# Double-buffered normalised rows, table and choice steps spread among other vector work, last scatters two tiles earlier, in a fused attention and mixture-of-experts kernel

## The chip, the core and the metric

The kernel runs on one core of a Trainium2 chip. Its time is the device time of one execution in microseconds (us), the median of several runs. Five engines work at once: PE (matrix products), DVE (vector), ACT (scalar functions), POOL (GpSimd, which here mostly issues indirect DMAs) and SP (which issues most other DMAs). Each engine takes its instructions in order; engines meet through semaphores, counters that one instruction raises and another waits for.

## The reference, cut to what matters

```
x = L0_attn_x                                   # 4 sequences x 1024 tokens x 128, f32
x = x + attention(layernorm(x), w_lhs, w_rhs)   # scores (x*w_lhs)(x*w_rhs)^T, softmax over 1024 tokens, times layernorm(x)
h2 = layernorm(x)
probs = softmax(h2 @ router_w.T)                # 8 experts
gates, chosen = top_2(probs); gates /= gates.sum()
for each token and each of its 2 experts e:
    y += gate_e * (gelu(h2 @ w_fc[e] + b_fc[e]) @ w_proj[e] + b_proj[e])   # 128 -> 512 -> 128
x = x + y
```

## The kernel before, in words

The attention runs sequence by sequence ("batch" b = 0..3) on 128-token tiles, eight to a batch, in two "units" of four tiles (unit u = 2b, 2b+1). The second half is the mixture of experts, and its rows are sorted by expert. For each token the normalised row h2 is written as a float16 high and low part into `stage`, together with its two gates, its first expert and its number. POOL scatters these rows with indirect DMAs (`dispatch`, line 846) into a table in DRAM called `slots`, where each expert has a region of its own. A batch takes 16 scatters: 8 tiles of tokens, 2 experts each.

The regions are then read back in 47 tiles: 24 full ones of 256 rows, then 23 of 128. Which region and row a tile starts at is computed on DVE by `make_table`, a generator whose yields are its steps, and which `steps(table, n)` advances by n steps. It runs four times: `first_table` (tiles 0 to 7), `second_table` (8 to 15), `late_table` (16 to 23) and `small_table` (24 on). `table_made` counts the finished ones.

A tile k passes through the engines like this.

- SP `load` fetches its rows. The loads of tiles 8 to 15 wait for all scatters of batch 2 (`dispatched[0]`) and for the second table; those of tiles 16 on wait for the 16 last scatters, batch 3's.
- PE in its step k: `turn_slots(k+2)` (4 transposes, line 1352), `up(k)` (12 matmuls, lines 1365 to 1367), `down(k-2)` (16 matmuls, line 1386). `down(k)` waits for `biased_made` to reach k-1, since it writes the PSUM bank that `add_bias(k-2)` reads. In step 4, behind `down(2)`, comes `rank_round(last)`, which counts how many tokens of batch 3 chose each expert; `up(5)` and `down(3)` follow.
- ACT copies the transposed rows out of PSUM, does the gelu, and in its first steps makes h2 of the last two units (`make_h2`, `high_h2`).
- DVE in its step k: `keep_rows(k)` (5 small operations on the rows' gates and numbers), `add_bias(k-3)` (line 1844, waits until `up(k)` is done and so until PE is past `down(k-3)`), and `gate(k-3)` (line 1851).
- POOL `give_back(k-4)` in step k scatters the gated rows to `results` (line 950), two indirect DMAs for a full tile, one for a half tile; 71 in all.

In its steps 0 to 5 DVE also carries the routing of batch 3: statistics of unit 7 (`take_stats2`, `take_moments2`), `choose` (the generator `picks`, lines 1594 to 1615, which ends in `taken_made`, and so lets `rank_round` start), `find_gap`, `split_h2` (the low part of h2, line 1565), the second table, `keep_ranks(last)` and `find_slots(last)`. The last line of `find_slots`, 1662, raises `meta_made`, for which the last scatters wait on POOL. The queue of POOL around this is written out by hand: scatters of batch 2 in groups of 5, 6, 4 and 1 with other work between them, then the tiles' steps, with eight of the last scatters in step 6 and eight in step 7 (`LAST_SCATTERS`), ahead of that step's `give_back`.

At the end SP loads `results` once the results of all tiles are returned, DVE adds them to x, and x is stored.

Of the kernel before, what the change touches and what calls it, by code (L numbers as in the profile page):

```python
# [8 lines left out]
P = 128  # L9
F32 = mybir.dt.float32  # L10
# [13 lines left out]
def preln_attention_moe(nc, x, w_lhs, w_rhs, router_wT, w_fc, b_fc, w_proj, b_proj, out):  # L24
# [69 lines left out]
    with ExitStack() as ctx:  # L94
# [65 lines left out]
        h2 = sb("h2", [P, TU, D], F32)  # L160
# [580 lines left out]
        def _(pool):  # L741
# [201 lines left out]
            LAST_SCATTERS = {6: range(0, 8), 7: range(8, SCATTERS)}  # L943
# [21 lines left out]
        def _(act):  # L965
# [35 lines left out]
            def make_h2(u, t):  # L1001
# [7 lines left out]
                act.activation(h2[:, t, :], res[:, n, :], ACT.Identity, bias=bias, scale=scale).then_inc(h2_made, 1)  # L1009

            def high_h2(u):
# [6 lines left out]
                act.activation(high, h2[:, :, :], ACT.Copy).then_inc(h2hi_made, 1)  # L1018
# [79 lines left out]
            def step(k, a):  # L1098
# [320 lines left out]
        def _(dve):  # L1419
# [128 lines left out]
            def take_moments2(u):  # L1548
# [5 lines left out]
                ins.then_inc(ln2_moments, 1)  # L1554
                dve.wait_ge(ln2_moments, u + 1)
# [4 lines left out]
            def split_h2(u):  # L1560
# [4 lines left out]
                dve.tensor_tensor(part[:, :, D:2 * D], h2[:, :, :], part[:, :, 0:D], ALU.subtract).then_inc(h2lo_made, 1)  # L1565
# [73 lines left out]
            def find_slots(r):  # L1639
# [3 lines left out]
                for k in range(K):  # L1643
                    route_link(dve.tensor_tensor(pick[k][:, mine, :], pick[k][:, mine, :], rank[:, mine, :], ALU.mult))
                route_settle()
                for k in range(K):
                    ins = dve.tensor_reduce(slot_f[:, mine, k], pick[k][:, mine, :], AX_X, ALU.add)
                ins.then_inc(slots_made, 1)
                dve.wait_ge(slots_made, 4 * r + 1)
                dve.tensor_copy(slot[:, at, :], slot_f[:, mine, :]).then_inc(slots_made, 1)  # L1650
                dve.wait_ge(gate_exp, r + 1)
                route_link(dve.tensor_scalar(gate_sum[:, mine], gate2[:, mine], 1.0, None, ALU.add))
                route_settle()
                if b >= 2:
                    dve.wait_ge(dispatched[b % 2], 16 * K * BT * (b // 2))
                dve.reciprocal(rows[:, :, GATES], gate_sum[:, mine]).then_inc(slots_made, 1)
                dve.wait_ge(slots_made, 4 * r + 3)
                dve.tensor_tensor(rows[:, :, GATES + 1], rows[:, :, GATES], gate2[:, mine], ALU.mult).then_inc(slots_made, 1)
                dve.wait_ge(slots_made, 4 * r + 4)
# [26 lines left out]
            for b in range(B):  # L1686
# [86 lines left out]
                if b == B - 1:  # L1773
                    find_slots(ROUNDS_BY[b - 1] - 1)
# [41 lines left out]
            digits = {}  # L1816

            def keep_rows(k, a):
# [4 lines left out]
                if k >= NR:  # L1823
# [6 lines left out]
                                         op0=ALU.is_equal, op1=ALU.mult)  # L1830
                dve.scalar_tensor_tensor(out=gate_parts[:, a, 1, 0:n], in0=first_expert, scalar=e, in1=slot_rows[:, :, GATES + 1],
                                         op0=ALU.not_equal, op1=ALU.mult)
                dve.scalar_tensor_tensor(out=chosen_row[:, a, 0:n], in0=first_expert, scalar=e, in1=slot_rows[:, :, NUMBER],
# [93 lines left out]
```

## Time and profile before

| | |
|---|---|
| time, median of 3 runs | 307.52 us (306.63 to 308.74) |
| the profiled execution | 307.93 us, of which the span shown is 306.4 us |
| mean granted clock of PE in it | 0.964 of full speed |
| busy | PE 88%, DVE 77%, ACT 64%, POOL 59% |

The profiled execution is one of the runs' kind, 0.4 us above their median. Times in rows are us from the span's start. In rows that follow an engine through time ("timeline"), the columns are start, duration, engine, line of the code, operation, out<-in with sizes, and the count; a bracket at the end gives the engine's idle time just before the row and what ended it. Consecutive instructions of one form are joined into one row.

### The profile page before, as it was taken

Reading aid. Unit: us, or ns where it says so; the run is one execution under the profiler, and the core shown is the slowest. Engines: PE = TensorE matmul, PEld = TensorE weight load, DVE = VectorE, ACT = ScalarE, POOL = GpSimd, SP = SyncE. Lnnn points to the kernel's source line nnn. Section 1 sums busy time; section 2 is a strip of 40 time slices with the busy share of each in tenths; the row PEclk is TensorE's granted clock in tenths of the full one; section 3 lists DMA queues with packets and bytes.
Section 4 is the critical chain, followed back from the end, with each engine's and each line's share of the span. In section 5 each row is a group of like instructions: output and inputs, shape, how many; then the busy total and the mean of one; then the engine's idle time right before and its main releaser. Section 6 shows DMA issues by size and latency. Waiting matters only on the chain.

```text
span 306.4 us, 8241 instructions
## 1 busy us (share of the span) xinstructions
PE 270.9 (88%) x2223; PEld 242.1 (79%) x2223; DVE 236.1 (77%) x1002; ACT 196.4 (64%) x427; POOL 180.6 (59%) x245
## 2 busy tenths in 40 slices
PE   7899999899989998899989499988999999999500
PEld 2479898788969887689879499978999999998500
DVE  4699898889878769988979988897665655676655
ACT  2447378896369772545776667675778887898300
POOL 8111036017577782787757857777777777766600
PEclk9999999999999999999999689999999999999955
DMA  6960000000401100111241152213333333221886
GB/s 195 415 282 4 0 3 0 3 0 0 143 26 56 45 18 20 37 44 37 79 136 45 37 136 88 72 46 108 106 92 95 100 97 90 80 64 46 318 283 272
DMA packets 15450, 28.51 MB, mean 93 GB/s; under 512 B 3904, under 2 KB 9920, under 8 KB 15152
## 3 DMA queue, kind: packets, MB, share of 16 engines
q1 hardware_dynamic: 10224, 16.88, 16.8%
q0 software_dynamic: 4608, 10.07, 9.9%
q10 hardware_dynamic: 576, 1.05, 1.0%
q8 instruction: 20, 0.33, 0.4%
q14 instruction: 22, 0.18, 0.2%
HBM read 15.83 MB, written 12.16 MB: 91 GB/s over the span
## 4 chain that ended last, share of the span: by engine, by line
PE 56%; DVE 26%; issue 5%; ACT 5%; POOL 3%; DMA 3%; DVEq 1%; SPq 0%; POOLq 0%; ACTq 0%
PE av_ps L1386 16%; PE av_ps L1181 14%; DVE neg_piece L1502 5%; PE sc_ps L1365 3%; PE sc_ps L1367 3%; PE sc_ps L1366 3%; DMA raw_proj<-results 2%; PE sc_ps L1170 2%; PE bank L1352 2%; DVE h_all L1844 2%; PE bank L1157 2%; PE bank L1159 1%; PE bank L1158 1%; ACT h_all L972 1%; PE sc_ps L1158 1%
## 5 line engine op out<-in xcount | busy, mean ns | idle before, releaser
L950 POOL DMA_INDIRECT results<-prob,result_row x71 | 68.7, 968 | 27.4 <-issue 10.4
L1094 ACT ACTIVATE raw_fc<-sc_ps,bfc,scale_down 128x128 f32<-128x128 f32 (+1 forms) x188 | 81.6, 530 | 0.8 <-PE sc_ps L1367 0.8
L1386 PE MATMUL av_ps<-raw_proj,raw_fc 128*128 x568 | 74.5, 283 | 5.9 <-DVE h_all L1844 5.7
L846 POOL DMA_INDIRECT slots<-stage,slot x64 | 63.8, 997 | 25.7 <-issue 18.9
L1386 PEld LDWEIGHTS av_ps<-raw_proj,raw_fc 128*128 128x128 f32 x568 | 68.6, 196 | 8.0 <-issue 7.6
L1181 PE MATMUL av_ps<-h_all,prob 128*128 128x137 f32 x512 | 73.2, 285 | 0.6 <-DVE lg_part L1533 0.5
L1181 PEld LDWEIGHTS av_ps<-h_all,prob 128*128 128x128 f32 x512 | 66.8, 190 | 4.4 <-DVE res L1530 1.6
L1365 PE MATMUL sc_ps<-h_all,wfc_hi 128*128 128x128 f16 (+1 forms) x188 | 43.5, 248 | 1.1 <-ACT raw_fc L1094 1.1
L1366 PE MATMUL sc_ps<-h_all,wfc_hi 128*128 128x128 f16 (+1 forms) x188 | 43.5, 248 | 0.0
L1367 PE MATMUL sc_ps<-h_all,wfc_lo 128*128 128x128 f16 (+1 forms) x188 | 43.4, 247 | 0.0
L1844 DVE TENSOR_TENSOR h_all<-av_ps,bpr 128x256 f32<-128x256 f32 (+1 forms) x47 | 16.9, 360 | 28.7 <-PE sc_ps L1367 24.8
L1086 ACT ACTIVATE h_all<-bank 128x512 f16<-128x512 f16 (+1 forms) x47 | 23.4, 501 | 23.8 <-PE sc_ps L1367 23.3
L1502 DVE TENSOR_REDUCE neg_piece<-bank 128x1 f32<-128x512 f32 x32 | 22.0, 688 | 7.3 <-PE sc_ps L1170 3.5
L999 ACT ACTIVATE prob<-sc_ps 128x512 f32<-128x512 f32 x32 | 18.1, 599 | 10.0 <-PE sc_ps L1170 9.9
L989 ACT ACTIVATE again<-bank 128x512 f32<-128x512 f32 x16 | 9.6, 597 | 22.0 <-DVE neg_piece L1502 22.0
L1502 DVE TENSOR_REDUCE neg_piece<-sc_ps 128x1 f32<-128x512 f32 x32 | 21.9, 684 | 1.1 <-PE sc_ps L1159 1.0
L1365 PEld LDWEIGHTS sc_ps<-h_all,wfc_hi 128*128 x188 | 18.5, 98 | 2.8 <-issue 1.3
L1851 DVE TENSOR_SCALAR prob<-h_all,row_gate 128x128 f32<-128x128 f32 x71 | 19.1, 309 | 1.7
L1009 ACT ACTIVATE h<-res,shift,rstd 128x128 f32<-128x128 f32 x32 | 14.7, 489 | 8.3 <-DVE stage L1565 4.8
L1367 PEld LDWEIGHTS sc_ps<-h_all,wfc_lo 128*128 x188 | 18.5, 98 | 1.3
L1366 PEld LDWEIGHTS sc_ps<-h_all,wfc_hi 128*128 x188 | 18.5, 98 | 0.9
L1157 PE MATMUL bank<-hT_hi,q_hi 128*128 128x512 f32 x32 | 14.3, 448 | 1.6 <-DVE h_all L1461 1.3
(201 smaller groups left out, 524.5 us busy)
## 6 DMA issues: line engine op xcount, KB each, us to landing
slots_in<-slots SPq DMA_DIRECT2D x24, 132.0 KB
raw_fc<-in_w_fc_dram SPq DMA_DIRECT2D x1, 2048.0 KB, 10.9
raw_proj<-in_w_proj_dram SPq DMA_DIRECT2D x1, 2048.0 KB, 15.2
res<-in_x_dram SPq DMA_DIRECT2D x3, 512.0 KB, 5.8
slots_in<-slots SPq DMA_DIRECT2D x23, 66.0 KB
results<-prob,result_row POOLq DMA_INDIRECT x71, 2.3
slots<-raw_fc POOLq DMA_DIRECT2D x2, 528.0 KB, 4.1
slots<-stage,slot POOLq DMA_INDIRECT x64, 2.3
```

Source lines behind the costliest of these rows:

```text
L846: pool.indirect_dma_start(out=slots[:, :], out_offset=bass.IndirectOffsetOnAxis(ap=slot[:, n, k:k + 1], axis=0), in_=stage[:, b % 2, t, :] ...
L950: pool.indirect_dma_start(out=results[:, :], out_offset=bass.IndirectOffsetOnAxis(ap=result_row[a][:, h:h + 1], axis=0), in_=gated[a][h], ...
L1086: act.activation(xT[:, a % NH, 0:n], bank[a % 2][:, :].bitcast(F16)[:, 0:n], ACT.Copy).then_inc(xT_made, 1)
L1094: ins = act.activation(hid[:, a % NH, c, 0:halves_of(k) * P], up_ps(k, c), ACT.Gelu_apprx_tanh, bias=bfc[:, e, c:c + 1], scale=scale_down[ ...
L1157: pe.matmul(o, q_hi[:, a, rows], hT_hi[:, a, cols], start=True, stop=False, skip_group_check=True)
L1181: mm = pe.matmul(att[:, t, 0:AUG], probT[:, m % RING, t * P:(t + 1) * P], h_aug[:, b % 2, exp_rows(n), :], start=(n % BT == 0 and t % 2 == ...
L1365: pe.matmul(o, wfc_hi[:, e, of], xT[:, a % NH, 0:w], start=True, stop=False, skip_group_check=True)
L1366: pe.matmul(o, wfc_hi[:, e, of], xT[:, a % NH, w:2 * w], start=False, stop=False, skip_group_check=True)
L1367: mm = pe.matmul(o, wfc_lo[:, e, of], xT[:, a % NH, 0:w], start=False, stop=True, skip_group_check=True)
L1386: mm = pe.matmul(o, hid[:, a % NH, c, rows], wpr[:, e, c, :], start=(c == 0 and h == 0), stop=(c == HC - 1), skip_group_check=True)
L1502: dve.tensor_reduce(neg_piece[:, r // TU, r % TU, c:c + 1], block_bank(n), AX_X, ALU.max, negate=True).then_inc(max_made, 1)
L1844: dve.tensor_tensor(y, o, bpr[:, bass.ds(e, 1), :].to_broadcast([P, n, D]), ALU.add).then_inc(biased_made, 1)
```

## The change

1. `h2` gets two buffers, one for even and one for odd units. `make_h2(u)` waits for `split_h2(u-2)` in place of `split_h2(u-1)`; unit 7's four `make_h2` go two each to ACT's steps 2 and 3 (before, one each to steps 2 to 5).
2. DVE: `second_table` starts earlier, one step at a time inside `find_slots` of batch 2's last round and the statistics of units 6 and 7, and ends in step 0 (before, in step 4). The first read of the experts' numbers (`load_experts(0)`) moves ahead of `add_attention`. `choose` runs one step at a time between the operations of `keep_rows(1)` and `keep_rows(2)`. `find_gap(last)` comes at the end of step 2 and `split_h2(6)` at the start of step 2.
3. DVE, steps 3 to 5: `add_bias(k-3)` and `gate(k-3)` stand ahead of `keep_rows(k)`; in step 5 also ahead of `keep_ranks(last)` and `find_slots(last)`. `split_h2(7)` goes from step 7 to step 5. The late and small tables run one step at a time among `keep_rows` and `gate` of steps 6 to 9 and 10 to 13.
4. POOL: the scatters of batch 2 are grouped 6, 6, 3, 1, and the last 16 scatters come in steps 4 and 5, so `give_back(0)` follows the first eight and `give_back(1)` all sixteen.

The diff, cut to its core:

```diff
-        h2 = sb("h2", [P, TU, D], F32)
+        h2 = sb("h2", [P, 2, TU, D], F32)
...
-            for i in range(5):
+            for i in range(6):
                 dispatch(B - 2, i)
             scale_ln2(2 * B - 2)
-            for i in range(5, 11):
+            for i in range(6, 12):
                 dispatch(B - 2, i)
             scale_ln2(2 * B - 1)
-            for i in range(11, 15):
+            for i in range(12, 15):
                 dispatch(B - 2, i)
             gate_powers(len(ROUNDS) - 1)
...
-            LAST_SCATTERS = {6: range(0, 8), 7: range(8, SCATTERS)}
+            LAST_SCATTERS = {4: range(0, 8), 5: range(8, SCATTERS)}
...
-                if u >= 1:
-                    act.wait_ge(h2lo_made, u)
+                if u >= 2:
+                    act.wait_ge(h2lo_made, u - 1)
...
-                if 2 <= k < 6:
-                    make_h2(2 * B - 1, k - 2)
-                    if k == 5:
+                if 2 <= k < 4:
+                    for t in range(2 * k - 4, 2 * k - 2):
+                        make_h2(2 * B - 1, t)
+                    if k == 3:
                         high_h2(2 * B - 1)
...
-            def take_stats2(u):
+            def take_stats2(u, between=nothing):
                 dve.wait_ge(res_made, u + 1)
                 for t in range(TU):
+                    between()
                     ins = dve.bn_stats(stats2[:, u % 2, t, :], res[:, token_tile(u, t), :])
...
-            def find_slots(r):
+            def find_slots(r, between=nothing):
...
+                between()
                 route_settle()
                 for k in range(K):
                     ins = dve.tensor_reduce(slot_f[:, mine, k], pick[k][:, mine, :], AX_X, ALU.add)
                 ins.then_inc(slots_made, 1)
+                between()
...
                 if b == B - 1:
-                    find_slots(ROUNDS_BY[b - 1] - 1)
+                    dve.wait_ge(table_made, 1)
+                    second_table = make_table(dve, note, settle, 1)
+
+                    def second():
+                        steps(second_table, 1)
+                    find_slots(ROUNDS_BY[b - 1] - 1, second)
...
-                    take_stats2(2 * b)
-                    take_moments2(2 * b)
+                    take_stats2(2 * b, second)
+                    take_moments2(2 * b, second)
                     add_logits(2 * b)
 
-            dve.wait_ge(table_made, 1)
-            second_table = make_table(dve, note, settle, 1)
             steps(second_table, 8)
+            digits = {}
+            load_experts = expert_loader(dve, digits)
+            load_experts(0)
             add_attention(2 * B - 1)
...
+            STEPS = {0: second_table, 1: choose, 2: choose, 6: late_table, 7: late_table, 8: late_table, 9: late_table,
+                     10: small_table, 11: small_table, 12: small_table, 13: small_table}
+
+            def beside(k, n=1):
+                if k in STEPS:
+                    steps(STEPS[k], n)
...
                 if k == 0:
-                    take_stats2(2 * B - 1)
-                    take_moments2(2 * B - 1)
-                if 1 <= k < 4:
-                    steps(choose, (5, 5, 3)[k - 1])
-                if k == 3:
-                    find_gap(last)
+                    take_stats2(2 * B - 1, second)
+                    take_moments2(2 * B - 1, second)
+                if k == 2:
                     split_h2(2 * B - 2)
-                if k < 5:
-                    steps(second_table, (5, 6, 6, 4, 30)[k])
+                if 3 <= k < 6:
+                    add_bias(k - 3, (a - 3) % NB)
+                    gate(k - 3, (a - 3) % NB)
                 if k == 5:
                     keep_ranks(last)
                     find_slots(last)
-                if k == 7:
                     split_h2(2 * B - 1)
-                if 6 <= k < 10:
-                    steps(late_table, (7, 10, 10, 30)[k - 6])
-                if 10 <= k < 14:
-                    steps(small_table, (9, 9, 9, 30)[k - 10])
                 if tile_there(k):
                     keep_rows(k, a)
-                if k >= 3:
+                if k >= 6:
                     add_bias(k - 3, (a - 3) % NB)
+                    beside(k)
                     gate(k - 3, (a - 3) % NB)
+                beside(k, {0: 30, 1: 3, 2: 12, 6: 3, 7: 3, 8: 3, 9: 40, 13: 40}.get(k, 3))
+                if k == 2:
+                    find_gap(last)
```

The order that comes out on the engines, at three places. First, DVE around `keep_rows(0)` and `keep_rows(1)`. Before, `keep_rows` stands in one piece (the rows that write gate_parts, chosen_row, row_gate and result_row), then five steps of the choice (best, pick0, first_id0):

```order
L1829 SCALAR_TENSOR_TENSOR gate_parts<-slots_in,of_expert 128x2
L1831 SCALAR_TENSOR_TENSOR gate_parts<-slots_in,of_expert 128x2
L1833 SCALAR_TENSOR_TENSOR chosen_row<-slots_in,of_expert 128x2
L1836 TENSOR_TENSOR row_gate<-gate_parts 128x2
L1837 TENSOR_TENSOR result_row0<-chosen_row,spare_row 128x2
L1594 TENSOR_REDUCE best<-lg 128x8
L1597 TENSOR_TENSOR pick0<-lg,best 128x64
L1600 SCALAR_TENSOR_TENSOR pick0<-pick0,expert_id 128x64
L1604 TENSOR_REDUCE first_id0<-pick0 128x8
```

Now, in `keep_rows(1)`, the two alternate:

```order
L1853 SCALAR_TENSOR_TENSOR gate_parts<-slots_in,of_expert 128x2
L1601 TENSOR_REDUCE best<-lg 128x8
L1856 SCALAR_TENSOR_TENSOR gate_parts<-slots_in,of_expert 128x2
L1604 TENSOR_TENSOR pick0<-lg,best 128x64
L1859 SCALAR_TENSOR_TENSOR chosen_row<-slots_in,of_expert 128x2
L1607 SCALAR_TENSOR_TENSOR pick0<-pick0,expert_id 128x64
L1863 TENSOR_TENSOR row_gate<-gate_parts 128x2
L1611 TENSOR_REDUCE first_id0<-pick0 128x8
L1865 TENSOR_TENSOR result_row1<-chosen_row,spare_row 128x2
```

Each step of the choice needs the one before it, and now has an operation of `keep_rows` between itself and that one; in `keep_rows(0)` the steps between are the second table's.

Second, DVE from the gap of batch 3's gates (gap) to the first biases (h_all). Before:

```order
L1626 TENSOR_TENSOR gap<-step_down,rstd2 128x8
L1565 TENSOR_TENSOR stage<-h2,stage 128x4x128
L560 SCALAR_TENSOR_TENSOR tile_row<-sums,tile_at 128x8
L564 TENSOR_TENSOR of_expert<-of_expert,second_lane 128x8
L566 TENSOR_TENSOR tile_last<-tile_row,sums 128x8
L569 TENSOR_TENSOR skipped<-tile_row,tile_last 128x8
L1829 SCALAR_TENSOR_TENSOR gate_parts<-slots_in,of_expert 128x2
...
L1837 TENSOR_TENSOR result_row3<-chosen_row,spare_row 128x2
L1844 TENSOR_TENSOR h_all<-av_ps,bpr 128x256
```

Now:

```order
L1633 TENSOR_TENSOR gap<-step_down,rstd2 128x8
L1872 TENSOR_TENSOR h_all<-av_ps,bpr 128x256
L1880 TENSOR_SCALAR prob<-h_all,row_gate 128x128 x2
L1853 SCALAR_TENSOR_TENSOR gate_parts<-slots_in,of_expert 128x2
```

The split of h2, four table steps and `keep_rows(3)` no longer stand between the gap and `add_bias(0)`: the first two come earlier, the third behind it.

Third, POOL from the end of batch 2's scatters on (slots is a scatter of rows, results a `give_back`, gate<-euler,gap the gates of batch 3; the last number is the count). Before:

```order
L846 DMA slots<-stage,slot 32768x132 x4
L855 TENSOR_TENSOR gate<-euler,gap 128x8
L846 DMA slots<-stage,slot 32768x132
L950 DMA results<-prob,result_row 22528x128 x4
L846 DMA slots<-stage,slot 32768x132 x8
L950 DMA results<-prob,result_row 22528x128 x2
L846 DMA slots<-stage,slot 32768x132 x8
L950 DMA results<-prob,result_row 22528x128 x65
```

Now:

```order
L846 DMA slots<-stage,slot 32768x132 x3
L855 TENSOR_TENSOR gate<-euler,gap 128x8
L846 DMA slots<-stage,slot 32768x132 x9
L950 DMA results<-prob,result_row 22528x128 x2
L846 DMA slots<-stage,slot 32768x132 x8
L950 DMA results<-prob,result_row 22528x128 x69
```

The first of the last sixteen scatters now follows batch 2's last one directly, where four give-backs stood between; the number of calls is the same.

## Rows read from the trace of the kernel before

**Rows 1.** The page, busy time of each engine, its share of the span, instructions.
```profile
PE 270.9 (88%) x2223; PEld 242.1 (79%) x2223; DVE 236.1 (77%) x1002; ACT 196.4 (64%) x427; POOL 180.6 (59%) x245
```

**Rows 2.** Timeline of POOL, from 154 us to its last call.
```profile
154.83 0.19 POOL L802 TENSOR_SCALAR neg_mean<-moments 128x4 f32<-128x4 f32 x1 [2.13 <-DVE moments L1553]
...
173.45 1.03 POOL L846 DMA_INDIRECT slots<-stage,slot  x1 [0.20 <-issue]
...
181.96 0.96 POOL L846 DMA_INDIRECT slots<-stage,slot  x1 [0.30 <-issue]
...
267.45 0.96 POOL L950 DMA_INDIRECT results<-prob,result_row  x1 [0.30 <-issue]
...
290.52 1.02 POOL L950 DMA_INDIRECT results<-prob,result_row  x1 [0.30 <-issue]
```

**Rows 3.** Timeline of DVE, line 1851: the gate of the last tile.
```profile
288.50 0.28 DVE L1851 TENSOR_SCALAR prob<-h_all,row_gate 128x128 f32<-128x128 f32 x1
```

**Rows 4.** Timeline of PE, 172 to 210 us.
```profile
172.74 3.77 PE L1386 MATMUL av_ps<-raw_proj,raw_fc 128*128 x16 [4.24 <-DVE h_all L1844]
178.99 1.95 PE L1386 MATMUL av_ps<-raw_proj,raw_fc 128*128 x16
180.78 0.39 PE L1352 MATMUL bank<-ident,slots_in 128*128 128x128 f16 x4
...
182.31 1.95 PE L1386 MATMUL av_ps<-raw_proj,raw_fc 128*128 x16
...
207.63 2.05 PE L1386 MATMUL av_ps<-raw_proj,raw_fc 128*128 x16 [1.49 <-DVE h_all L1844]
209.51 0.39 PE L1352 MATMUL bank<-ident,slots_in 128*128 128x128 f16 x4
```

**Rows 5.** Windows of 1 us: PE, PEld, DVE, ACT, POOL busy, PEclk, DMA, GB/s.
```profile
171.00:172.00 1.00, 0.00 (x0) 0.00 (x0) 0.93 (x7) 1.00 (x3) 0.97 (x2) 0.72 0.00 0
...
178.00:179.00 1.00, 1.00 (x10) 0.87 (x9) 0.88 (x7) 0.00 (x0) 0.00 (x0) 0.86 0.45 165
```

**Rows 6.** Timeline of DVE, 171 to 179 us.
```profile
171.28 0.21 DVE L1829 SCALAR_TENSOR_TENSOR gate_parts<-slots_in,of_expert 128x2 f32<-128x2 f32 x1
...
172.08 0.43 DVE L1844 TENSOR_TENSOR h_all<-av_ps,bpr 128x256 f32<-128x256 f32 x1
...
172.94 0.17 DVE L572 TENSOR_TENSOR spare_row<-skipped,place 128x16 f32<-128x16 f32 x1
...
174.38 0.21 DVE L1829 SCALAR_TENSOR_TENSOR gate_parts<-slots_in,of_expert 128x2 f32<-128x2 f32 x1
...
176.91 0.23 DVE L1634 TENSOR_TENSOR rank<-av_ps,next_slot 128x64 f32<-128x64 f32 x1 [0.80 <-PE av_ps L1209]
...
178.83 0.17 DVE L1662 COPY stage<-row_id 128x8 f32<-128x8 f32 x1
```

**Rows 7.** Timeline of DVE, 152 to 161 us.
```profile
152.71 0.17 DVE L1661 TENSOR_SCALAR stage<-first_id 128x4 f32<-128x4 f32 x1
152.79 0.16 DVE L1662 COPY stage<-row_id 128x4 f32<-128x4 f32 x1
...
155.17 0.17 DVE L475 TENSOR_SCALAR tiles<-count 128x8 f32<-128x8 f32 x1
155.38 0.17 DVE L479 TENSOR_SCALAR tiles<-tiles 128x8 f32<-128x8 f32 x1
...
157.30 0.18 DVE L1526 RECIPROCAL inv_sum<-av_ps 128x4 f32<-128x4 f32 x1 [0.74 <-PE av_ps L1181]
...
159.71 0.87 DVE L1545 BATCH_NORM_STATS2 stats<-res 128x6 f32<-128x128 f32 x4 [0.74 <-issue]
```

**Rows 8.** Timeline of ACT, at line 1009.
```profile
170.82 0.49 ACT L1009 ACTIVATE h<-res,shift,rstd 128x128 f32<-128x128 f32 x1 [4.83 <-DVE stage L1565]
```

**Rows 9.** Timeline of SP's queue: the loads of tiles 8 to 15 and of 16 to 19.
```profile
176.57 15.01 SPq L723 DMA_DIRECT2D slots_in<-slots  x8
...
207.21 5.54 SPq L723 DMA_DIRECT2D slots_in<-slots  x4
```

More of the change, by code:

```diff
@@ L1017, in high_h2 @@
                 high = stage[:, b % 2, (u % 2) * TU:(u % 2 + 1) * TU, :].bitcast(F16)[:, :, 0:D]
-                act.activation(high, h2[:, :, :], ACT.Copy).then_inc(h2hi_made, 1)
+                act.activation(high, h2[:, u % 2, :, :], ACT.Copy).then_inc(h2hi_made, 1)
             def split_weights(i):
@@ L1540, in add_logits, with nothing, take_moments2 @@
                 dve.tensor_tensor(lg[:, at, :], lg_part[:, :, :], x_logits[:, b % 2, at, :], ALU.add).then_inc(lg_made, 1)
-            def take_stats2(u):
+            def nothing():
+                pass
+            def take_stats2(u, between=nothing):
                 dve.wait_ge(res_made, u + 1)
                 for t in range(TU):
+                    between()
                     ins = dve.bn_stats(stats2[:, u % 2, t, :], res[:, token_tile(u, t), :])
                 ins.then_inc(ln2_stats, 1)
-            def take_moments2(u):
+            def take_moments2(u, between=nothing):
+                between()
                 dve.wait_ge(ln2_stats, u + 1)
@@ L1564, in split_h2 @@
                 part = stage[:, b % 2, (u % 2) * TU:(u % 2 + 1) * TU, :].bitcast(F16)
-                dve.tensor_tensor(part[:, :, D:2 * D], h2[:, :, :], part[:, :, 0:D], ALU.subtract).then_inc(h2lo_made, 1)
+                dve.tensor_tensor(part[:, :, D:2 * D], h2[:, u % 2, :, :], part[:, :, 0:D], ALU.subtract).then_inc(h2lo_made, 1)
             done = [0]
@@ L1644, in find_slots @@
                     route_link(dve.tensor_tensor(pick[k][:, mine, :], pick[k][:, mine, :], rank[:, mine, :], ALU.mult))
+                between()
                 route_settle()
@@ L1648, in find_slots @@
                 ins.then_inc(slots_made, 1)
+                between()
                 dve.wait_ge(slots_made, 4 * r + 1)
@@ L1652, in find_slots @@
                 route_link(dve.tensor_scalar(gate_sum[:, mine], gate2[:, mine], 1.0, None, ALU.add))
+                between()
                 route_settle()
@@ L1656, in find_slots @@
                 dve.reciprocal(rows[:, :, GATES], gate_sum[:, mine]).then_inc(slots_made, 1)
+                between()
                 dve.wait_ge(slots_made, 4 * r + 3)
                 dve.tensor_tensor(rows[:, :, GATES + 1], rows[:, :, GATES], gate2[:, mine], ALU.mult).then_inc(slots_made, 1)
+                between()
                 dve.wait_ge(slots_made, 4 * r + 4)
@@ L1850, in gate @@
                 for h in range(halves_of(k)):
+                    beside(k + 3)
                     ins = dve.tensor_scalar(gated[k % NR][h], biased[:, a % NH, h, :], row_gate[:, a, h:h + 1], None, ALU.mult)
@@ L1868, in step @@
                     find_slots(last)
-                if k == 7:
                     split_h2(2 * B - 1)
-                if 6 <= k < 10:
-                    steps(late_table, (7, 10, 10, 30)[k - 6])
-                if 10 <= k < 14:
-                    steps(small_table, (9, 9, 9, 30)[k - 10])
                 if tile_there(k):
                     keep_rows(k, a)
-                if k >= 3:
+                if k >= 6:
                     add_bias(k - 3, (a - 3) % NB)
+                    beside(k)
                     gate(k - 3, (a - 3) % NB)
-            run_each_tile(expert_loader(dve, digits), step, 3, lambda group: dve.wait_ge(table_made, group + 1))
+                beside(k, {0: 30, 1: 3, 2: 12, 6: 3, 7: 3, 8: 3, 9: 40, 13: 40}.get(k, 3))
+                if k == 2:
+                    find_gap(last)
+            run_each_tile(load_experts, step, 3, lambda group: dve.wait_ge(table_made, group + 1))
             for u in range(2 * B):
```

6 lines of the change are left out of this document (4 added, 2 removed).

## The prediction

> **What bounds the kernel now.** I read the busy shares first [rows 1]. PE is busiest, with 88%, POOL has 59%; that is an average over stages, so it doesn't say what sets the end. The timeline of POOL does, for the second half [rows 2]: from the first of the last scatters, 181.96, to the call at 267.45 there are 68 calls, 67 intervals in 85.49 us, 1.276 us each, which is 0.96 us of a call and 0.30 us to the next one. POOL has no idle time there: it is the bound. The 15 intervals after that take 23.07 us in place of 15 x 1.276 = 19.1, so there it waits 3.9 us for tiles. The last tile's gate ends at 288.78 [rows 3], the last call starts at 290.52; from there to the end of the span is 15.9 us of landing, loads, additions and stores, which the change leaves alone.
>
> So what matters is when POOL's saturated stretch begins, and whether tiles come fast enough to keep it full to the end. Both go back to one stop of PE. It ends its matmuls of `up(4)` at 172.74 - 4.24 = 168.50 and waits for the first biases [rows 4], which DVE writes from 172.08 on [rows 6]. During that stop the granted clock falls to its half level: the mean of 0.72 from 171 to 172 says that it fell within that us, and the 0.86 from 178 to 179 that it came back within this one [rows 5]. So PE takes 178.99 - 172.74 = 6.25 us from `down(2)` to `down(3)`. At full clock that is a step, 182.31 - 178.99 = 3.32 [rows 4], and the rank round, some small matmuls, which I put at 0.3, near the 0.39 of four transposes: 3.6. The stop costs 4.2 and the half clock 2.6 more. `meta_made`, which lets the last scatters start, comes at 179.0 [rows 6].
>
> **DVE, 155 to 172.** A small step that needs the one before starts 0.205 us after it (155.17, 155.38), one that doesn't 0.08 after it (152.71, 152.79) [rows 7]. So an operation set between two dependent ones saves between 0 and 0.125. Before unit 7's statistics stand 11 more table steps and the read of the experts' numbers. The read had 0.74 of its own ahead of 159.71; now it falls partly into the 0.74 in which DVE waits for PE ahead of 157.30 [rows 7]. The 11 steps, spread among other work, push that wait out and some 0.5 more. Statistics start 0.2 earlier, at 159.5.
>
> From there to the first biases: before, 172.08 - 159.71 = 12.4 us. Out go the 11 steps at 0.18 (eight in a row take 174.38 - 172.94 = 1.44), 2.0, and `keep_rows(3)`, 172.08 - 171.28 = 0.8 [rows 6]. In come the table's last eight, 1.44. Ten table steps and eight of the choice now stand between other operations; I take 0.1 saved for each, 1.8, since 0.205 less 0.08 is 0.125 and not each slot is free. `add_bias(0)` starts at 159.5 + 12.4 - 2.0 - 0.8 + 1.44 - 1.8 = 168.7. With nothing saved it would be 170.5; before 168.5 PE isn't there.
>
> **PE at that place.** Biases end 0.43 later, PE starts 0.2 after that (172.51 to 172.74), so `down(2)` goes at 169.4: an idle time of 0.9 in place of 4.2. PE had one of 1.49 elsewhere [rows 4], with no drop of clock behind it (its `down` there takes 2.05, as against 3.77 at the half clock). So the clock stays, and `up(5)`, done by 178.99 before, is done at 169.4 + 3.6 = 173.0. Six us earlier.
>
> **The last scatters.** In step 5 DVE now does `add_bias(2)`, which waits for `up(5)`, and its gate (0.9 together) and then keep_ranks and find_slots, 179.0 - 176.91 = 2.1 [rows 6]: behind the waiting instruction is exactly what POOL needs. `meta_made` at 173.0 + 0.9 + 2.1 = 176.0, the first scatter at 176.4. Ahead of it POOL is free: the scatters of batch 2 end earlier, since the sixth goes into the idle 2.13 ahead of 154.83 [rows 2].
>
> From 176.4 POOL has 87 calls in a row, 16 scatters and 71 give-backs, four of which stood ahead before. 86 x 1.276 = 109.7, so the last starts at **286.1**, in place of 290.52: 4.4 less. It needs tiles in time.
>
> **PE afterwards.** PE reaches `turn_slots(8)`, at 180.78 before [rows 4], at 173.0 + 1.8 = 174.8. Tile 8's load waits for batch 2's last scatter. That stood at 173.45; now one scatter less follows the idle time (-1.27), while unit 6's moments come 0.3 later, so 172.5. The load went 3.1 after it [rows 2, 9]: 175.6, and some 2.0 for landing, 177.6. PE waits 2.8 there and is ahead by 3.2 instead of 6. From 182.31 to 207.63 it had lost 25.32 - 7 x 3.32 = 2.1 us to late biases, as the table steps of steps 9 to 13 stood ahead of them [rows 4]; spread out, they should no longer be late: ahead by 5.3 at tile 16, 204.2. That load waits for the last of the 16 scatters, the 18th call: 176.4 + 17 x 1.27 = 198.0; before, the load at 207.21 [rows 9] was 3.7 behind 181.96 + 17 x 1.27 = 203.5, so 201.7 and landing by 204.0, just in time. The last gate comes at 288.5 - 5.3 = 283.2, 2.9 before POOL's last call: POOL bounds to the end.
>
> **What costs nothing.** The ACT wait of 4.83 for the one h2 buffer [rows 8] goes. It ran beside PE's own stop, which hid it, so I put its own gain at 0; with that stop down to 0.9 the wait would show, by up to the 3.3 that the stop shrinks. `split_h2(7)`, before in step 7, follows `meta_made` and is needed only by the second eight scatters, 10 calls later.
>
> **Sum.** 307.93 - 4.4 = 303.5 for the profiled execution, which stands 0.4 over the median of 307.52; on the median's footing 303.1. I say **303.2**.
>
> **A rule against it.** Rows 7 show 0.205 and 0.08. The Trainium skill, "VectorE: DVE Perf Modes", section "The DRAIN you can't avoid", says that chained vector operations cost the same with a semaphore after each as with one after the last, since the next can't start until the pipe has emptied. By that rule spreading steps out saves nothing, and it would be the slower rival below. The trace speaks against it for these small operations.
>
> **Rivals.**
>
> *Slower: spreading saves nothing.* Then `add_bias(0)` starts 1.8 later, and the 11 early steps push their full 2.0 instead of 0.5: 168.7 + 1.8 + 1.5 = 172.0. PE stops as long as before, the clock falls, `up(5)` is done at 178.9, and now the last scatters wait behind `add_bias(2)`: 178.9 + 3.0 + 0.4 = 182.3. With four more calls behind it, POOL ends at 182.3 + 109.7 = 292.0, 1.5 later than before: 309.4. It decides from a first scatter at 290.52 - 109.7 = 180.8 on; from 183.9 on it is 3.1 slower. For it: DVE has hardly an idle time from 161 on. Against it: rows 7. Chance 0.09.
>
> *The clock falls in the new wait for tile 8.* An idle time of 1.49 kept it, one of 4.24 didn't; 2.8 lies between. If it falls, PE loses up to the same 2.6 and is ahead by 2.7 at the end; then PE, not POOL, sets the end: 307.9 - 2.7 = 305.2, between 304.6 and 306.5. Against it: the stop before began at 168.50 and lost the clock only in the us from 171, and this one is shorter [rows 4, 5]. Chance 0.22. On this the Trainium skill, "TensorE: Matmul & The Clock Gate", section "HAM oscillation — how this bites in real kernels", says that a long enough wait for a DMA returns PE to the half clock, as the stop here shows.
>
> *No gain.* The change doesn't do all it says: biases at 170.5 or a load of tile 8 two us later, so PE is ahead by a step less. First scatter at 179 to 180, the end at 306.5 to 308.5. Chance 0.11.
>
> *More.* First scatter near 175.4 and intervals of 1.266, as most single ones are: below 302.3. Chance 0.08.
>
> The forecast, 302.3 to 304.6, has 0.5.
>
> **How the numbers follow.** 1%, 3.1 us, is what a measurement of this kernel can tell: faster means below 304.4. That holds nearly all of the forecast (0.48), "more" (0.08) and a little of the clock rival (0.02): 0.58. Slower than 310.6 needs a first scatter past 183.9: part of the first rival and a mishap in tile 16's load, 0.07. The rest, 0.35. The range from 301.8 to 306.8 holds the forecast, the clock rival, half of "more" and a little of "no gain", 0.8.
>
> **What would show it.** First biases at 168 to 170; PE's stop before `down(2)` under 2 us and a full clock from 171 to 178; the first scatter of the last 16 at 175.4 to 178; a wait of PE of 2 to 3 us ahead of the transposes of tile 8, with the clock held or not; no stop near 200 for biases; POOL without idle time up to its last call, near 286. If POOL has idle time after 250, PE is the bound and a rival holds; if its intervals are longer than 1.3, my price for a call is wrong.

## The result, and the profile after

The changed kernel takes 305.57 us (median of 13 runs, 304.18 to 307.04), the kernel before 307.52 beside it: ratio 0.993, 95% interval 0.9909 to 0.9951. That is 2 us faster where 4.4 were forecast: a gain clear of the noise and inside the range, but short of the 304.4 below which the prediction called the kernel faster.

In the profiled execution (305.57 us, span 304.0) DVE's busy time is what the change shortened, from 236.1 us [rows 1] to 229.5, with the same 1002 instructions:

```profile
PE 269.3 (89%) x2223; PEld 240.0 (79%) x2223; DVE 229.5 (75%) x1002; ACT 196.4 (65%) x427; POOL 180.6 (59%) x245
```

The timeline of PE, at the places of [rows 4]:

```profile
169.30 2.05 PE L1387 MATMUL av_ps<-raw_proj,raw_fc 128*128 x16 [0.88 <-ACT raw_fc L1094]
...
174.90 2.05 PE L1387 MATMUL av_ps<-raw_proj,raw_fc 128*128 x16 [1.77 <-issue]
...
177.59 0.40 PE L1353 MATMUL bank<-ident,slots_in 128*128 128x128 f16 x4 [0.64 <-DMA slots_in<-slots]
...
206.32 0.40 PE L1353 MATMUL bank<-ident,slots_in 128*128 128x128 f16 x4 [1.59 <-DMA slots_in<-slots]
```

The stop of 4.24 is 0.88, `down(2)` takes 2.05 and not 3.77: the half clock is gone. The window of 1 us in which it fell before, columns as in [rows 5], now has the full clock:

```profile
171.00:172.00 1.00, 1.00 (x21) 0.95 (x20) 0.93 (x7) 1.00 (x4) 1.00 (x1) 1.00 0.19 63
```

The first of PE's rows names ACT as what ended the stop, but `down(2)` needs only the gelu of tile 2, which ACT had done at 165.91 (the one of tile 3 ends at 169.22). It is the biases that it waits for: they end at 169.06, and PE starts 0.24 behind them, as before. Three waits are left: 1.77 ahead of `down(3)`, 0.64 for tile 8, 1.59 for tile 16. PE leads by 180.78 - 177.59 = 3.2 us at tile 8, and still by 209.51 - 206.32 = 3.2 at tile 16.

The timeline of POOL, as in [rows 2]: batch 2's last scatter, the first and the last two of the 16, the last calls.

```profile
172.31 1.03 POOL L846 DMA_INDIRECT slots<-stage,slot  x1 [0.19 <-issue]
177.15 0.95 POOL L846 DMA_INDIRECT slots<-stage,slot  x1 [3.81 <-DVE stage L1572]
...
197.36 1.30 POOL L846 DMA_INDIRECT slots<-stage,slot  x1 [0.31 <-issue]
198.96 1.22 POOL L846 DMA_INDIRECT slots<-stage,slot  x1 [0.30 <-issue]
...
282.75 0.96 POOL L950 DMA_INDIRECT results<-prob,result_row  x1 [0.30 <-issue]
284.50 0.96 POOL L950 DMA_INDIRECT results<-prob,result_row  x1 [0.78 <-DVE prob L1880]
285.76 1.36 POOL L950 DMA_INDIRECT results<-prob,result_row  x1 [0.30 <-DVE prob L1880]
287.43 1.02 POOL L950 DMA_INDIRECT results<-prob,result_row  x1 [0.30 <-issue]
```

The timeline of DVE: the first biases, `add_bias(2)`, the last line of `find_slots`, the last gate.

```profile
168.64 0.42 DVE L1872 TENSOR_TENSOR h_all<-av_ps,bpr 128x256 f32<-128x256 f32 x1
...
173.43 0.42 DVE L1872 TENSOR_TENSOR h_all<-av_ps,bpr 128x256 f32<-128x256 f32 x1 [1.47 <-PE sc_ps L1368]
...
176.20 0.17 DVE L1674 COPY stage<-row_id 128x8 f32<-128x8 f32 x1
...
285.40 0.29 DVE L1880 TENSOR_SCALAR prob<-h_all,row_gate 128x128 f32<-128x128 f32 x1
```

From 177.15 to 282.75 POOL runs without idle time beyond the 0.30 between calls, 83 intervals of 1.272; then it waits once more for a gate. Two calls at the last scatters take 1.30 and 1.22 in place of 0.96. The timeline of DVE beside them:

```profile
197.26 0.56 DVE L528 TENSOR_TENSOR past<-tile_id,per_expert 128x384 f32<-128x384 f32 x1 [0.46 <-DVE per_expert L525]
...
198.79 0.56 DVE L544 TENSOR_TENSOR past<-of_expert,lane 128x384 f32<-128x384 f32 x1
199.39 0.96 DVE L548 TENSOR_TENSOR chosen<-past,per_expert 128x768 f32<-128x768 f32 x1
```

And SP's queue, the load of tile 16:

```profile
203.07 0.33 SPq L723 DMA_DIRECT2D slots_in<-slots  x1
```

Three wide operations of the small table, each on two tensors, start just ahead of a call or run beside it; tile 16's load goes 203.07 - 198.96 = 4.1 us after the last scatter's start.

### The profile page after: what moved, and what is told of

Read it like the earlier page. It is cut to its first block, busy times and chain, and to the rows that moved or that the text cites. A ratio compares the mean times of both kernels' runs of the same rounds, so it can differ in the third digit from the quotient of the medians.

```text
span 304.0 us, 8244 instructions
## 1 busy us (share of the span) xinstructions
PE 269.3 (89%) x2223; PEld 240.0 (79%) x2223; DVE 229.5 (75%) x1002; ACT 196.4 (65%) x427; POOL 180.6 (59%) x245
## 4 chain that ended last, share of the span: by engine, by line
PE 50%; POOL 14%; issue 13%; DVE 9%; DMA 7%; ACT 5%; SPq 1%; POOLq 0%; DVEq 0%; ACTq 0%
PE av_ps L1387 15%; PE av_ps L1182 11%; POOL slots L846 10%; PE sc_ps L1366 4%; PE sc_ps L1368 3%; PE sc_ps L1367 3%; DVE neg_piece L1503 3%; DMA raw_proj<-results 3%; DMA slots<-stage,slot 2%; DMA slots_in<-slots 2%; PE bank L1353 2%; PE sc_ps L1171 2%; PE bank L1158 1%; ACT h_all L972 1%; PE bank L1160 1%
## 5 line engine op out<-in xcount | busy, mean ns | idle before, releaser
L846 POOL DMA_INDIRECT slots<-stage,slot x64 | 64.1, 1002 | 29.2 <-issue 18.9
L1387 PE MATMUL av_ps<-raw_proj,raw_fc 128*128 x568 | 72.7, 278 | 2.8 <-issue 1.9
L1387 PEld LDWEIGHTS av_ps<-raw_proj,raw_fc 128*128 128x128 f32 x568 | 67.0, 192 | 4.9 <-issue 4.5
L1353 PE MATMUL bank<-ident,slots_in 128*128 128x128 f16 x142 | 15.3, 219 | 2.2 <-DMA slots_in<-slots 2.2
```

Source lines behind the costliest of these rows:

```text
L846: pool.indirect_dma_start(out=slots[:, :], out_offset=bass.IndirectOffsetOnAxis(ap=slot[:, n, k:k + 1], axis=0), in_=stage[:, b % 2, t, :] ...
L1353: mm = pe.transpose(o[:, part * w + h * P:part * w + (h + 1) * P], x, ident16[:, :])
L1387: mm = pe.matmul(o, hid[:, a % NH, c, rows], wpr[:, e, c, :], start=(c == 0 and h == 0), stop=(c == HC - 1), skip_group_check=True)
```

## The experiments

Ratios are to the kernel before, with their 95% intervals. **Theory 1**: PE's lead at tiles 8 and 16, which their loads hold back, and the start of POOL's stream set the end. Where an expectation below names another theory 1 (runs 1, 7 and 8), its own is meant; the rivals stand with each run.

**1. No spreading.** The same steps at the same places, but each group in one piece:

```diff
-                    find_slots(ROUNDS_BY[b - 1] - 1, second)
+                    find_slots(ROUNDS_BY[b - 1] - 1)
+                    steps(second_table, 5)
...
             def beside(k, n=1):
-                if k in STEPS:
+                if k in STEPS and (k >= 3 or n > 1):
```

> The changed kernel, with the steps of the second table and of the choice in the same places but each group in one piece ahead of or behind the other work, not between its operations (11 ahead of add_attention, 10 around unit 7's statistics and keep_rows(0), 8 of the choice). Theory 1 (a dependent step that waits costs 0.205, one that fills another's wait 0.08 to 0.13): 29 steps cost some 0.1 more each, the first biases start near 171.5 (168.64), PE stops for 3.5 us or more ahead of down(2) and its clock falls; first scatter near 182, time 308 to 309; if the clock holds, first scatter near 180, time 307. Rival (what a chained step costs doesn't depend on a wait): biases stay at 168.7, time 305.6.

309.46 us, ratio 1.005 (1.0023 to 1.0076). The timeline of DVE at the first biases:

```profile
171.89 0.42 DVE L1874 TENSOR_TENSOR h_all<-av_ps,bpr 128x256 f32<-128x256 f32 x1
```

And of PE behind them:

```profile
172.56 2.05 PE L1387 MATMUL av_ps<-raw_proj,raw_fc 128*128 x16 [3.27 <-DVE h_all L1874]
```

The biases start at 171.89 in place of 168.64: 3.25 us for 29 steps, 0.11 each. Without spreading nothing of the gain is left: 3.9 us lie between the two medians. The chain of the choice goes no faster when spread, 0.26 us from best to pick0 (164.56, 164.82) against 0.25 before (162.52, 162.77); the operation that now stands in its gap is the one that comes free. The Trainium skill, "VectorE: DVE Perf Modes", section "The DRAIN you can't avoid", has eight chained copies cost the same with a semaphore after each as with one after the last, and adds that a next operation that isn't held starts earlier. The trace shows such early starts: where choice and `keep_rows(1)` alternate, operations of 0.21 us start 0.13 to 0.14 apart. The prediction's rule against spreading leaves that addition out.

The first scatter came at 180.41, as the line for a clock that holds had it. In this execution (307.58 us, 2.0 over the changed kernel's profiled one) it did hold, behind the stop of 3.27:

```profile
172.00:173.00 1.00, 0.44 (x4) 0.45 (x5) 0.96 (x5) 1.00 (x3) 1.00 (x1) 1.00 0.00 0
```

Eight of the ten runs took 308.7 to 310.3, with mean clocks of 0.963 to 0.971 against 0.974 and 0.975 in the two faster ones. So part of the 3.9 us may be a clock that fell in most runs, which no profile shows.

**2. The ranks ahead of the wait.** 

```diff
+                if k == 5:
+                    keep_ranks(last)
+                    find_slots(last)
                 if 3 <= k < 6:
                     add_bias(k - 3, (a - 3) % NB)
                     gate(k - 3, (a - 3) % NB)
                 if k == 5:
-                    keep_ranks(last)
-                    find_slots(last)
                     split_h2(2 * B - 1)
```

> The changed kernel, with keep_ranks(last) and find_slots(last) of DVE's step 5 ahead of add_bias(2) instead of behind it. Theory 1 (the start of the last 16 scatters, and through the last of them tile 16's load, sets the end): DVE no longer waits for up(5) before it, find_slots ends near 174.2, the first scatter starts near 174.6 (177.15 in the changed kernel); PE's 1.77 us ahead of down(3), which waits for ranks_kept, goes to under 0.5 and turns into a longer wait for tile 8 (2.4 in place of 0.64); tile 16 is turned by 205 (206.32), the last call starts near 285.3 (287.43); time 303.5. Rival, clock: the wait for tile 8 of 2.4 us lowers the clock, PE loses up to 2.6, time 305 to 306. Rival, tail: the last call is earlier, but what follows it grows by as much, time 305 to 306 with the last call near 285.3.

303.69 us, ratio 0.9869 (0.9831 to 0.9906). Its timeline of PE:

```profile
173.04 1.95 PE L1387 MATMUL av_ps<-raw_proj,raw_fc 128*128 x16
...
177.79 0.44 PE L1353 MATMUL bank<-ident,slots_in 128*128 128x128 f16 x4 [2.80 <-DMA slots_in<-slots]
...
182.91 0.39 PE L1353 MATMUL bank<-ident,slots_in 128*128 128x128 f16 x4
```

And windows of 1 us, columns as in [rows 5]:

```profile
177.00:178.00 1.00, 0.21 (x4) 0.21 (x4) 0.38 (x4) 0.00 (x0) 0.69 (x2) 1.00 0.53 190
178.00:179.00 1.00, 0.93 (x8) 0.54 (x6) 0.00 (x0) 0.00 (x0) 0.69 (x2) 0.51 0.52 148
```

`down(3)` goes without its wait and the first scatter at 174.89, as expected. The wait for tile 8 grows to 2.80 and the clock falls to half behind it: the next step takes 182.91 - 177.79 = 5.12 us. In this execution the last call starts at 287.33, no earlier than now: the clock takes back what the earlier scatters give, as the rival said. The median is theory 1's all the same. Three of the six executions have a mean clock of 0.974 and took 302.6 to 303.2; three, the profiled one among them, have 0.963 to 0.969 and took 304.2 to 305.5. That fits a clock that falls in some executions only; the faster ones were not profiled.

**3. One give_back ahead of the scatters.** In POOL's step 4 the order is turned round:

```diff
-                for i in LAST_SCATTERS.get(k, ()):
-                    dispatch(B - 1, i)
+                if k != 4:
+                    for i in LAST_SCATTERS.get(k, ()):
+                        dispatch(B - 1, i)
...
                     give_back(k - 4, (k - 4) % NR)
+                if k == 4:
+                    for i in LAST_SCATTERS[4]:
+                        dispatch(B - 1, i)
```

> The changed kernel, with give_back(0) ahead of the first eight of the last scatters on POOL instead of behind them. Theory 1: its two calls run in POOL's idle 3.81 us (173.6 to 176.1), the first scatter still starts near 177.2, the last one near 196.4 instead of 198.96; tile 16 is turned without a wait near 204.7 (206.32 after a wait of 1.59), the last call starts near 285.2, time 303.4. Rival, tail: last call as early, time unchanged at 305.6. Rival, the two calls hold up the first scatter by a call: last scatter 197.7, time 304.5.

303.25 us, ratio 0.9861 (0.9831 to 0.989). Its timeline of POOL:

```profile
174.94 0.96 POOL L950 DMA_INDIRECT results<-prob,result_row  x1 [0.30 <-issue]
177.39 0.95 POOL L846 DMA_INDIRECT slots<-stage,slot  x1 [1.50 <-DVE stage L1576]
...
196.33 0.96 POOL L846 DMA_INDIRECT slots<-stage,slot  x1 [0.30 <-issue]
```

And of PE at tile 16:

```profile
204.75 0.39 PE L1357 MATMUL bank<-ident,slots_in 128*128 128x128 f16 x4
```

All as theory 1 had it: no wait at tile 16, the last call at 285.65. Two calls, moved into idle time, are worth what the forecast missed, 2.3 us. The move does two things at once: POOL's stream is two calls shorter, and PE leads by 209.51 - 204.75 = 4.8 in place of 3.2. The stream alone would have reached its last call at 177.39 + 84 x 1.272 = 284.2; POOL waited for gates near the end (idle 0.81 and 0.92), so here PE came last.

**4. All of that, and batch 2's last scatter sooner.** 2 and 3, and `gate_powers` behind that scatter:

```diff
-            for i in range(12, 15):
-                dispatch(B - 2, i)
-            gate_powers(len(ROUNDS) - 1)
-            for i in range(15, SCATTERS):
+            for i in range(12, SCATTERS):
                 dispatch(B - 2, i)
+            gate_powers(len(ROUNDS) - 1)
```

> The changed kernel, with three moves: keep_ranks(last) and find_slots(last) ahead of add_bias(2), give_back(0) ahead of the first eight of the last scatters, and gate_powers behind batch 2's last scatter instead of ahead of it. Theory 1 (the loads of tiles 8 and 16 set PE's lead, the stream of calls the end): batch 2's last scatter starts near 170.7 (172.31), tile 8 is turned near 176.0 (177.59) after a wait of about 1 us, too short for the clock to fall as it did in the 2.80 of the kernel with the ranks alone; last scatter near 195.3, tile 16 without a wait near 202.6; last gate near 281.7, last call near 283, time 300.3 (299.5 to 301.5). Rival (POOL's stream alone counts): 85 calls from a first scatter near 176.2 end near 283 too, but with gates after it. Rival, tail: last call near 283, time 302 or more.

301.16 us, ratio 0.9802 (0.9789 to 0.9816): the fastest version, 6 us under the kernel before. The profiled execution was 1.5 us late already at 151 us, ahead of all that differs (the same operation at 152.82, at 151.28 in the changed kernel). Less that, tile 8 is turned at 176.0 after a wait of 1.04 that keeps the clock, tile 16 at 203.0, and the last call starts at 283.95. What the third move brings by itself was not run.

**5. The last scatters' place.** Back in steps 6 and 7:

```diff
-            LAST_SCATTERS = {4: range(0, 8), 5: range(8, SCATTERS)}
+            LAST_SCATTERS = {6: range(0, 8), 7: range(8, SCATTERS)}
```

> The changed kernel, with the last scatters in POOL's steps 6 and 7 again: give_backs 0 and 1 run ahead of them, give_back(2) between. Theory 1 (PE's lead at tile 16 counts): POOL gets through four calls before 178.7, but the last scatter starts only near 200.3, tile 16's load lands 1.4 us later than now, PE waits 3.0 us for it and is ahead of the kernel before by 1.8; last call near 288.8, time 307. Rival (POOL's number of calls counts): its stream starts near 173.6 in place of 177.15, last call near 284 to 285, time 303 to 304.

304.69 us, ratio 0.9912 (0.9879 to 0.9945); the last scatter at 200.65 as expected, but tile 16's wait is 1.54, not 3.0, as its load goes 3.03 behind the scatter and not 4.1. Theory 1 misses by 2.3 us, the rival by 0.7; the last call, 287.61, lies between them. The rows speak for PE's lead all the same. POOL's stream of calls starts 3.4 us earlier than in the changed kernel, PE leads at tile 16 by 209.51 - 206.44 = 3.1 as there, and the last gate comes when it did (285.40). POOL, PE and DVE in turn:

```profile
173.76 0.96 POOL L950 DMA_INDIRECT results<-prob,result_row  x1 [0.30 <-issue]
206.44 0.40 PE L1353 MATMUL bank<-ident,slots_in 128*128 128x128 f16 x4 [1.54 <-DMA slots_in<-slots]
285.58 0.29 DVE L1880 TENSOR_SCALAR prob<-h_all,row_gate 128x128 f32<-128x128 f32 x1
```

What POOL had gained it lost in waits from 264 us on. And in the kernel before, that line alone the other way round:

> The kernel before, with one line of the change: the last scatters in POOL's steps 4 and 5. Theory 1 (without an earlier PE and DVE the move brings nothing): the first of the 16 starts near 179.8, some 0.9 behind find_slots (181.96 before), the last near 201.3 (203.47), but PE's stop of 4.24, its half clock and its later waits for biases stay, the last gate at 288.5 and the last call at 290.5 too, time 307.5 within 1. Rival (the scatters' place is what counts): last call 2.2 earlier, time 305.3.

307.37 us, ratio 0.9991 (0.9973 to 1.0009), the first of the 16 at 180.03, the last call at 291.00. So the move of the scatters, undone or alone, changes nothing that can be measured.

**6. One h2 buffer.**

```diff
-                if u >= 2:
-                    act.wait_ge(h2lo_made, u - 1)
+                if u >= 1:
+                    act.wait_ge(h2lo_made, u)
```

> The changed kernel, with one h2 buffer again, and make_h2(7) waiting for split_h2(6). Theory 1 (split_h2(6) now comes early, so the second buffer carries little): ACT's make_h2(7) at 166.04 waits till 166.96, its step 3 is 0.9 later, PE starts down(2) at 169.3 and down(3) at 174.9 as now; first scatter at 177.2, time 305.6, within 0.5. Rival (as the prediction put it, the wait of ACT shows by up to 3.3 us once PE's stop is short): down(3) and up(5) later by 1 to 3 us, time 307 to 308.5.

304.67 us, ratio 0.9932 (0.9909 to 0.9954). The timeline of ACT:

```profile
167.40 0.88 ACT L1009 ACTIVATE h<-res,shift,rstd 128x128 f32<-128x128 f32 x2 [1.12 <-DVE stage L1572]
```

ACT waits 1.12 where 4.83 stood, and nobody waits for it: PE's idle times ahead of `down(2)` and `down(3)` are 0.88 and 1.77 as now. What took the old wait away is the early `split_h2(6)`, not the second buffer.

**7. What holds POOL's calls.** `split_h2(7)` sooner:

> The changed kernel, with split_h2(7) (a subtraction of two tensors, 0.68 us) at the head of DVE's step 5, in its wait for up(5), in place of right behind find_slots. Theory 1 (POOL can't prepare a call while DVE subtracts two tensors): the first scatter, which starts at 177.15 where the subtraction ends at 176.96, starts 0.2 behind the last operation of find_slots, near 176.5, the last scatter near 198.2, last call near 286.9, time 305.0. Rival (POOL needs 0.8 us from the semaphore to its first call): first scatter stays 0.8 behind find_slots, near 177.1, time 305.6.

304.78 us, ratio 0.9927 (0.9912 to 0.9943). The rival holds: `find_slots` ends at 176.43, the first scatter starts at 177.21, 0.8 behind it with nothing between. That the last call (286.90) and the time still come out near theory 1's has another reason: in this execution the wide operations fell behind the calls, as in the last run below, and PE had no wait at tile 16. And the other form of the same operations:

> The changed kernel, with split_h2 and the last additions of the results written as scalar_tensor_tensor (times 1.0, then subtract or add) in place of tensor_tensor; same values, same sizes. Theory 1 (only tensor_tensor holds POOL back from preparing a call): the call at the first addition takes 0.96 in place of 1.36, the first scatter starts 0.6 earlier, calls beside split_h2 take 0.96 in place of 1.35, time 304.7. Rival (any operation with two operands in SBUF holds POOL back): calls as long as now, time 305.6.

304.59 us, ratio 0.9907 (0.9894 to 0.9921), too near the changed kernel's to decide; the rows do. The timeline of POOL:

```profile
287.80 1.39 POOL L950 DMA_INDIRECT results<-prob,result_row  x1 [0.30 <-DVE prob L1880]
```

And of DVE beside it:

```profile
287.67 0.68 DVE L1913 SCALAR_TENSOR_TENSOR res<-res,hT_hi 128x512 f32<-128x512 f32 x1
```

The rival holds again: the call waits out 0.4 us beside either form. The Trainium skill, "SBUF — State Buffer", section "SBUF: two separate sides", gives one port pair to DVE and GpSimd, held by a vector operation with two SBUF inputs; these calls agree. In this execution the wait for tile 16 was 2.15, and the clock fell behind it, as PE and the window of 1 us show:

```profile
206.96 0.61 PE L1353 MATMUL bank<-ident,slots_in 128*128 128x128 f16 x4 [2.15 <-DMA slots_in<-slots]
207.00:208.00 1.00, 1.00 (x8) 0.75 (x8) 0.00 (x0) 0.00 (x0) 0.83 (x1) 0.50 0.51 133
```

**8. The wide operations elsewhere.** The small table in steps 11 to 14, and the changed kernel unaltered beside it:

```diff
-                     10: small_table, 11: small_table, 12: small_table, 13: small_table}
+                     11: small_table, 12: small_table, 13: small_table, 14: small_table}
```

> The changed kernel, with the steps of the small table one tile later on DVE (steps 11 to 14 in place of 10 to 13), so that its three wide operations on two tensors (0.56, 0.56 and 0.96 us) no longer run beside the last two of the last 16 scatters. Theory 1 (those operations hold up POOL's calls and so tile 16's load): the last scatter starts near 198.6, its call takes 0.96, tile 16's load goes 3.0 to 3.2 behind it (4.11 in the changed kernel), PE turns tile 16 near 204.8 without a wait (206.32 after 1.59), the last gate comes near 283.8, the last call near 286.5, time 304.6. Rival (the load waits for the transfer itself): tile 16 is turned near 206 as now, time 305.6.

306.36 us, ratio 0.9962 (0.9937 to 0.9986). The mechanism is as theory 1 had it: the last scatter takes 0.95, the load goes 3.04 behind it, the wait for tile 16 falls to 0.57. The time isn't: PE now waits 1.26 for tile 17. From tile 16 on the kernel takes one tile of 256 rows and then two of 128 in turn, so tile 17 is the first that the small table places, and its load waits for that table. The table's last line, 608, comes at 208.77 and not 204.02, and the load goes at 209.69 and not 204.94. Waits of SP from 200 to 215 us (in all, times, longest), and PE at tile 17:

```profile
SPq L715 <- DVE tile_start L608: 5.4, 1, 5.4
211.71 0.29 PE L1353 MATMUL bank<-ident,slots_in 128*128 128x128 f16 x2 [1.26 <-DMA slots_in<-slots]
```

The later table moved the wait from tile 16 to tile 17. (This profiled execution, too, was 1.5 us late at 151 us.)

> The changed kernel once more, beside the two above. Both theories: 305.6 within 0.7, with executions whose wait at tile 16 takes the clock to its half level some 1.5 us above the others.

305.18 us, ratio 0.9933 (0.9907 to 0.9959). Its profiled execution took 304.15 us, and there the wide operations fell 0.1 us behind the calls' starts instead of ahead of them. The timeline of POOL in it:

```profile
197.46 0.96 POOL L846 DMA_INDIRECT slots<-stage,slot  x1 [0.30 <-issue]
198.73 0.95 POOL L846 DMA_INDIRECT slots<-stage,slot  x1 [0.30 <-issue]
...
286.56 1.13 POOL L950 DMA_INDIRECT results<-prob,result_row  x1 [0.30 <-issue]
```

Of DVE:

```profile
197.54 0.56 DVE L528 TENSOR_TENSOR past<-tile_id,per_expert 128x384 f32<-128x384 f32 x1 [0.46 <-DVE per_expert L525]
199.08 0.56 DVE L544 TENSOR_TENSOR past<-of_expert,lane 128x384 f32<-128x384 f32 x1
```

And of PE at tile 16:

```profile
204.83 0.39 PE L1353 MATMUL bank<-ident,slots_in 128*128 128x128 f16 x4
```

The same program, no long call among the scatters, the load 3.03 behind the scatter, no wait at tile 16, a lead of 4.7, the last gate at 283.73 in place of 285.40, POOL without a wait for gates up to its last call at 286.56: the end that was forecast, within 0.7 us.

## Why the prediction was wrong

**Right.** Biases at 168.7 (168.64; some of that is luck, as the statistics began at 159.75 and not 159.5, and the way from there took 8.89 us and not 9.24), an idle time of 0.9 (0.88), the clock held, `up(5)` at 173.0 (`add_bias(2)`, which waits for it, starts at 173.43), tile 8 turned at 177.6 (177.59), POOL without idle time, 1.276 a call (1.272, up to 282.75), give-backs waiting behind it. Run 1 shows that the gain needs the spreading on DVE; what `add_bias` ahead of `keep_rows` brings by itself was not run.

**The step that failed**: "ahead by 5.3 at tile 16, 204.2" with the load "landing by 204.0, just in time". PE got there at 204.73 and waited until 206.32. The landing was 2.3 later than worked out: the last scatter 1.0 (its stream began 0.75 late, and the call of 1.30 ahead of it made up the rest), the load's issue 0.4 (4.1 behind it; 3.0 to 3.2 in the nine runs whose last scatter took 0.96), and the landing 3.25 where I took the 2.3 that [rows 4, 9] bound it by. The sum had 0.2 of slack, and PE came 0.5 later than in it: the first or the last of the three was enough by itself. PE's lead stayed 3.2, the last gate came at 285.40 and not 283.2, and POOL ran dry at the end, which the prediction itself names as the sign that PE is the bound.

**The sizes.** Against the last call of 286.1: the first scatter +0.75 (177.15; I had given it 0.4 behind `find_slots`, without a row for it; it takes 0.78 to 0.79 in all ten profiles in which POOL stood waiting for it), the stream -0.3, the last three intervals +0.85, of which 0.5 is the wait for a gate, PE's lost lead, and 0.4 the call beside the first addition: 287.43. The rest, 0.7, lies after it: 16.57 us to the end where I took the 15.9 of before. In the other profiles that stretch is 15.1 to 16.3 with no order by kernel, so I put it down to the execution, which I haven't shown. So the wait at tile 16 is the step that failed, but not the whole miss: the first scatter's start was mis-sized by more than the 0.5 that the gates cost POOL in this execution. Where the wait was absent (the repeated run of 8) the kernel took 304.15, 1.4 less, 0.9 of it at the last call.

**Missed, and hidden.** `down(3)` waits for `ranks_kept`, and `keep_ranks(last)` now stands behind the wait for `up(5)`: 1.77 us of PE. I named what POOL gets from there and not that PE waits for it too. It cost nothing, since tile 8's load came later anyway, and it spared the clock: without it (run 2) the wait for tile 8 is the 2.80 that I forecast, and the clock falls. The clock rival's mechanism is real, one wait away, and the argument against it, that the new wait is shorter than the old, does not hold: waits of 2.15 and 2.80 lost the clock. That 305.57 lies in that rival's interval is a coincidence, since in the profiled execution the clock held. My reason for h2's second buffer was wrong (run 6).

**Open.** How often does the wait at tile 16 come? Nothing here settles it: of the six profiles with this order at that place, four have it (1.59, 1.67 with one buffer, 2.15 in the second form of run 7, 1.77 in run 1), two have none. The clock may fall behind it more often than the profiles show: the four slowest of the changed kernel's 13 executions (305.9 to 307.0) have mean clocks of 0.966 to 0.968, the others 0.971 to 0.976, and none of the four was profiled. The median of 305.4 over both sets of runs lies between the two profiled ones, 304.15 and 305.57; part of the spread is the 1.5 us that some executions lose ahead of 151 us, in runs 4 and 8 alike.

## What to carry to other kernels

A step that is "just in time" in a sum is a wait: price the gain with and without it, and look for a call or two that can be taken out from in front of the thing waited for, into idle time (run 3: 2 us for turning two lines round). When an instruction with a wait is put ahead of others, list every engine that waits for those others, not just the one the move is meant for. Steps of a dependent chain are cheap between the steps of another: measure the pair, not the step.

## What the runs showed of the hardware

- A DVE operation on two SBUF tensors that starts just ahead of an indirect DMA's call on POOL holds that call up: 0.96 us become 1.2 to 1.7. A load that waits for the scatter then goes 3.7 to 4.1 us after the call's start in place of 3.0 to 3.2. Started 0.1 us after the call (197.54, 197.46), it costs the call nothing, and itself takes its usual 0.56.
- The clock held in a stop of 3.27 us (run 1, the profiled execution) and fell in ones of 2.15 (run 7) and 2.80 (run 2): the length of the stop alone doesn't decide.
- From the end of DVE's last write to the first indirect call behind it, 0.8 us pass on an idle POOL (176.37 to 177.15); a call that follows another starts 0.30 after it.
